# Two VectorE steps of a retrieval stage moved to GpSimd: the normed rows at a tile's beginning, and the add of the normed output into x

## What is computed

```python
x = x + _layernorm(_L1_attn_ref(_layernorm(x, axis=-1), memory, ...), axis=-1)

def _L1_attn_ref(hidden, memory, Wq, Wk, Wv, Wo, log_beta, g_state, b_state, g_mem, b_mem):
    Q = layernorm(hidden, g_state, b_state) @ Wq.T
    ...
    for _ in range(3):
        scores = einsum('bhsd,hnd->bhsn', xi, K) * beta     # 8 heads, 256 memories
        w = entmax15(scores)                                # a threshold per row and head, squared
        xi = einsum('bhsn,hnd->bhsd', w, V)
    return xi.transpose(0, 2, 1, 3).reshape(B, S, H * hd) @ Wo.T
```

## Time and profile before

| | us |
|---|---|
| median of three runs | 1821.33 (1820.55 to 1825.54) |
| the profiled execution | 1821.18, its span 1819.4 |
| busy in the span: PE | 1564.8 (86%) |
| busy in the span: DVE | 1361.7 (75%) |
| busy in the span: ACT | 1150.3 (63%) |
| busy in the span: POOL | 756.4 (42%) |

### The profile page before, as it was taken

How to read it: one execution, slowest core, us unless ns; L and a number is a source line. 1 busy time by engine, 2 the same in 40 slices (tenths; PEclk the granted TensorE clock), 3 DMA queues, 4 the chain that set the end, 5 groups by cost and what they waited for, 6 DMA issues and landing times. The chain is left out here.

```text
span 1819.4 us, 25815 instructions
## 1 busy us (share of the span) xinstructions
PE 1564.8 (86%) x7434; PEld 1099.6 (60%) x7434; DVE 1361.7 (75%) x3568; ACT 1150.3 (63%) x2769; POOL 756.4 (42%) x2049
## 2 busy tenths in 40 slices
PE   5799999999857788887997789877779999999987
PEld 2545657465646667766776678666645556555554
DVE  6665757572359999999999999999644566766646
ACT  3333342412148999899998998899547565665630
POOL 3514224140136776777667776777410101001000
PEclk9799999998988989989998999899889999999989
DMA  5000000000110000000000000000000000000000
GB/s 230 1 1 1 1 1 1 1 1 0 55 57 1 1 1 1 1 1 1 1 1 1 1 1 1 1 1 1 1 0 1 1 1 1 1 13 1 13 1 23
DMA packets 6716, 19.21 MB, mean 11 GB/s; under 512 B 1072, under 2 KB 4144, under 8 KB 5296
## 3 DMA queue, kind: packets, MB, share of 16 engines
q1 hardware_dynamic: 6576, 17.58, 2.6%
HBM read 15.48 MB, written 2.10 MB: 10 GB/s over the span
## 5 line engine op out<-in xcount | busy, mean ns | idle before, releaser
L1361 DVE BATCH_NORM_STATS2 r_moments<-mem_arena 128x6 f32<-128x512 f32 x576 | 382.7, 683 | 4.4 <-ACT mem_arena L1649 4.3
L1649 ACT ACTIVATE mem_arena<-mem_arena,r_shift 128x256 f32<-128x256 f32 x792 | 351.2, 513 | 33.1 <-POOL r_shift L1554 33.1
L1717 PE MATMUL r_bank<-arena,r_wT 128*128 128x256 f32 x1024 | 228.4, 381 | 7.5 <-ACT mem_arena L1649 5.8
L1717 PEld LDWEIGHTS r_bank<-arena,r_wT 128*128 128x128 f32 x1024 | 192.0, 190 | 37.9 <-issue 13.1
L1734 PE MATMUL r_bank<-ident,mem_arena 128*128 128x128 f32 x576 | 107.9, 323 | 90.2 <-DVE mem_arena L1377 89.5
L1734 PEld LDWEIGHTS r_bank<-ident,mem_arena 128*128 128x128 f32 x576 | 81.9, 166 | 127.2 <-DVE mem_arena L1377 97.2
L1325 DVE MAX8 r_top<-r_bank 128x8 f32<-128x256 f32 x384 | 144.2, 416 | 14.5 <-PE r_bank L1717 14.0
L2275 ACT ACTIVATE arena<-arena,e_NM 128x512 f32<-128x512 f32 (+3 forms) x256 | 134.4, 559 | 29.2 <-DVE e_NM L1963 29.2
L1717 PE MATMUL r_bank<-arena,r_xnT 128*128 128x256 f32 x512 | 120.8, 396 | 19.9 <-ACT mem_arena L1649 19.1
L1963 DVE CUSTOM_DVE_ANT_0 arena<-e_banks,mask_q 128x512 f32<-128x512 f32 (+3 forms) x256 | 110.2, 485 | 29.7 <-PE e_banks L2480 29.3
L1361 DVE BATCH_NORM_STATS2 r_moments<-r_u 128x6 f32<-128x512 f32 x192 | 129.2, 684 | 2.8 <-ACT r_u L1649 2.6
(11 more groups left out here) (332 smaller groups left out, 3366.2 us busy)
## 6 DMA issues: line engine op xcount, KB each, us to landing
w<-in_w SPq DMA_DIRECT2D x3, 1024.0 KB, 14.3
out_x<-X SPq DMA_DIRECT2D x4, 512.0 KB, 2.9
X<-in_x SPq DMA_DIRECT2D x1, 1536.0 KB, 10.7
w_in<-in_w_in SPq DMA_DIRECT2D x1, 1156.0 KB, 6.5
mem_arena<-in_wq SPq DMA_DIRECT2D x1, 1024.0 KB, 17.1
mem_arena<-in_wo SPq DMA_DIRECT2D x1, 1024.0 KB, 20.9
gate<-in_gate SPq DMA_DIRECT2D x1, 1024.0 KB, 7.6
up<-in_up SPq DMA_DIRECT2D x1, 1024.0 KB, 9.6
```

The source lines that it names most:

```text
L1361: last = dve.bn_stats(moments[:, a.lane, 2 * p:2 * p + 2, :].rearrange("p two c -> p (two c)"), u[a.lane][:, 2 * p:2 * p + 2, :].rearrange ...
L1649: last = act.activation(u[a.lane][:, h, :], u[a.lane][:, h, :] if k else scores[:, h, :], ACT.Relu, bias=shift[:, a.lane, h:h + 1])
L1717: last = pe.matmul(scores[:, h, :], lhs, (G1 if a.first else G2)[:, h, i, :], start=i == 0, stop=i == 1)
```

## The change

POOL makes the normed rows: `tile_rstd` also makes minus the mean, `tile_rows` multiplies it by the inverse deviation, and one tensor_scalar gives X * rstd + (-mean * rstd). It stands in POOL's slot behind the third head of its weights. For tiles 0 to 11 POOL also adds the normed output into X (`add_rows`), in the same place; DVE still makes the normed output, and it waits for the former tile's add before it writes it. The last four tiles keep their add on DVE. The statistics for the block that follows wait for the first four adds. The semaphore `rstd_ready` goes, `onorm_ready` comes.

```diff
--- before.py
+++ after.py
@@ -1250,11 +1250,13 @@
         ors = sb("r_ors", [P, 1])
         onorm = sb("r_onorm", [P, D])
         one_eps = sb("r_one_eps", [P, 1])
+        minus_one = sb("r_minus_one", [P, 1])
+        off = sb("r_off", [P, LANES])
         eps_sq = sb("r_eps_sq", [P, 1])
 
         ready = sem("ready")
-        stats_ready, rstd_ready, xn_ready, xnT_in_psum, xnT_ready = (sem(n) for n in (
-            "stats_ready", "rstd_ready", "xn_ready", "xnT_in_psum", "xnT_ready"))
+        stats_ready, xn_ready, xnT_in_psum, xnT_ready, onorm_ready = (sem(n) for n in (
+            "stats_ready", "xn_ready", "xnT_in_psum", "xnT_ready", "onorm_ready"))
         scores_done, top_ready, centred, squared, sum2, sum4, sum8, mean_ready, msq_ready, gap_ready, room_ready = (
             sem(n) for n in ("scores_done", "top_ready", "centred", "squared", "sum2", "sum4", "sum8", "mean_ready",
                              "msq_ready", "gap_ready", "room_ready"))
@@ -1307,15 +1309,6 @@
                 dve.drain()
                 dve.bn_aggr(mv[:, a.lane, :], stats[:, a.lane, :]).then_inc(stats_ready, 1)
 
-            def tile_rows(a):
-                if not (a.live and a.first):
-                    return
-                dve.wait_ge(rstd_ready, of_tile(a))
-                if a.tile >= 2:
-                    dve.wait_ge(xnT_in_psum, a.tile - 1)
-                dve.tensor_scalar(xn[:, a.tile % 2, :], X[:, a.tile, :], mv[:, a.lane, 0:1], rstd[:, a.lane:a.lane + 1],
-                                  ALU.subtract, ALU.mult).then_inc(xn_ready, 1)
-
             def largest(a, *heads):
                 if not a.live:
                     return
@@ -1387,11 +1380,17 @@
                 if not (a.live and a.last):
                     return
                 dve.wait_ge(ors_ready, of_tile(a))
-                dve.tensor_scalar(onorm[:], out_rows(a), omv[:, 0:1], ors[:, 0:1], ALU.subtract, ALU.mult)
+                if 0 < a.tile <= ending:
+                    dve.wait_ge(x_ready, a.tile)
+                last = dve.tensor_scalar(onorm[:], out_rows(a), omv[:, 0:1], ors[:, 0:1], ALU.subtract, ALU.mult)
+                if a.tile < ending:
+                    last.then_inc(onorm_ready, 1)
+                    return
                 dve.drain()
                 dve.tensor_tensor(X[:, a.tile, :], X[:, a.tile, :], onorm[:], ALU.add).then_inc(x_ready, 1)
 
             def first_batch_stats():
+                dve.wait_ge(x_ready, TPB)
                 dve.drain()
                 for t in range(TPB):
                     dve.bn_stats(T["e_stats"][:, t, :], X[:, t, :])
@@ -1417,7 +1416,6 @@
                 invert(Unit(n - 6), 2)
                 take_moments(Unit(n - 5), 1, 1, 2)
                 weights(Unit(n - 7), 1, 2)
-                tile_rows(Unit(n - 2))
                 take_moments(Unit(n - 5), 1, 3)
                 invert(Unit(n - 5), 1)
                 weights(Unit(n - 7), 3)
@@ -1453,6 +1451,7 @@
         @block.gpsimd
         def _(pool):
             pool.memset(one_eps[:], 1.0 + EPS)
+            pool.memset(minus_one[:], -1.0)
             pool.memset(eps_sq[:], EPS * EPS)
             pool.memset(inv_n[:], 1.0 / NMEM)
             for k in range(TOP):
@@ -1471,7 +1470,19 @@
                 pool.drain()
                 pool.tensor_tensor(v, v, eps_sq[:], ALU.add)
                 pool.drain()
-                pool.tensor_tensor(rstd[:, a.lane:a.lane + 1], v, T["half_neg"][:, 0:1], ALU.pow).then_inc(rstd_ready, 1)
+                pool.tensor_tensor(off[:, a.lane:a.lane + 1], mv[:, a.lane, 0:1], minus_one[:], ALU.mult)
+                pool.tensor_tensor(rstd[:, a.lane:a.lane + 1], v, T["half_neg"][:, 0:1], ALU.pow)
+
+            def tile_rows(a):
+                if not (a.live and a.first):
+                    return
+                o, r = off[:, a.lane:a.lane + 1], rstd[:, a.lane:a.lane + 1]
+                pool.drain()
+                pool.tensor_tensor(o, o, r, ALU.mult)
+                if a.tile >= 2:
+                    pool.wait_ge(xnT_in_psum, a.tile - 1)
+                pool.drain()
+                pool.tensor_scalar(xn[:, a.tile % 2, :], X[:, a.tile, :], r, o, ALU.mult, ALU.add).then_inc(xn_ready, 1)
 
             def centre(a):
                 if not a.live:
@@ -1568,6 +1579,12 @@
                 pool.tensor_tensor(ove[:], omv[:, 1:2], T["eps"][:, 0:1], ALU.add)
                 pool.drain()
                 pool.tensor_tensor(ors[:], ove[:], T["half_neg"][:, 0:1], ALU.pow).then_inc(ors_ready, 1)
+
+            def add_rows(a):
+                if not (a.live and a.last and a.tile < ending):
+                    return
+                pool.wait_ge(onorm_ready, of_tile(a))
+                pool.tensor_tensor(X[:, a.tile, :], X[:, a.tile, :], onorm[:], ALU.add).then_inc(x_ready, 1)
 
             def first_batch_norms():
                 var, rstd, rms, mv = (T["e_" + n] for n in ("var", "rstd", "rms", "mv"))
@@ -1607,6 +1624,8 @@
                 newton(Unit(n - 3), 0)
                 if n - 5 != UNITS - 1:
                     weights(Unit(n - 5), 7)
+                tile_rows(Unit(n))
+                add_rows(Unit(n - 7))
                 second_moment(Unit(n - 4), 2)
                 centre(Unit(n - 2))
                 square(Unit(n - 2))
```

## The result

| | before | after |
|---|---|---|
| median, us | 1821.42 (4 runs) | 1844.45 (1843.25 to 1845.76, 4 runs) |
| profiled execution, its span | 1821.18, 1819.4 | 1843.7, 1841.9 |
| memory stage: first DVE row to the last add into X | 833.5 | 857.3 |
| busy in the span: DVE | 1361.7 | 1351.1 |
| busy in the span: POOL | 756.4 | 775.2 |

The ratio is 1.0122, 95% interval 1.0105 to 1.014: 23.0 us slower. DVE lost 10.6 us of work and POOL got 18.8, and neither sum is the result.

What follows compares the result with a forecast made beforehand. The bound was POOL's gapless chain from DVE's first moments through `centre`, for which DVE's `clear` waits. Normed rows 19.4, start 5.4 and add net 2.3 made 27.1 us; on 1821.3 that gave 1848.4 us, range 1838 to 1866.

Steps and rivals of the forecast that it cites:

- (a): DVE between maxima and `clear`: removing the normed rows, 0.45 us each, only lengthens a wait for POOL; gain 0.
- (b): POOL before the second moment: normed rows add 1.62 us in each of twelve tiles, 19.4 us slower.
- (c): Start of the memory stage: tile 0's normed rows stand behind four tiles' deviations on POOL; 5.4 us slower.
- (d): DVE before the moments that release POOL: losing the add gains 0.50 us in twelve tiles, 6.0 us.
- (e): POOL's gapless stretch before `centre`: the add costs 0.69 us in twelve tiles, 8.3 us; net of DVE's gain 2.3.
- (f): PE's `output` waits for POOL's add, 2 to 3.7 us; transposes 0.8 us late, room 1.1 us; charged 0.
- Rival 2: PE turns late by the new wait or half clock: 5 to 18 us more, about 1860 us; 18%.
- The first: Rival: DVE is the bound and POOL's added work fits its idle time, 1815.3 us; 3%.
- The third: Rival: two scalars make POOL's normed rows cost 1.75 us instead of 1.14, 1856.3 us; 10%.
- The fourth: Rival: POOL's normed rows partly covered by the maxima, or the ramp overlaps, 1829 us; 7%.
- the fifth: Rival: the work moves without effect, for instance since `clear` waits anyway, 1821 us; 2%.
- What would show it: Signs in the later profile: DVE idle about 2.1 us before `clear`, periods of 17.3 us in slots with normed rows.

Runs made afterwards that it cites:

- rows_in_gap: Normed rows on POOL moved behind `start`, into a POOL wait, add on DVE, against the kernel before the change: ratio 1.0015, 2.7 us slower.
- add_in_gap: Only the add on POOL, moved behind its first head of weights, normed rows on DVE, against the kernel before: 1814.04 us against 1823.92, ratio 0.9948.
- warm_output_half: Changed kernel plus 6 or 3 dummy matmuls on PE ahead of its wait for the add: 1842.17 us, ratio 1.0111 to the kernel before.
- pe_waits_onorm: Changed kernel, but PE's `output` waits for DVE's normed output instead of POOL's add: 1841.27 us, ratio 1.0102 to the kernel before.

## Why the prediction was right

1848.4 us were forecast, 1844.45 came, in the range and with the sign; 27.1 us against 23.0. By its steps:

- **(a) DVE's normed rows give 0**: right, shown by rows_in_gap. I expected the 0.45 us as idle time at `clear` and found them there.
- **(b) normed rows on POOL, 19.4 us**: the mechanism was right, the size was not. This is the term that was mis-sized: 1.62 us per tile, measured 1.07, 12.8 us in all. The step that was off is "I take 1.14, the nearest row". The row was the same engine and shape but had max as its second operation; the true price was 0.55, far nearer to the lower bound of 0.438 than to the upper. 12 x 0.59 us too much from this, 12 x 0.04 too little for the drains.
- **(c) the start, 5.4 us**: 5.3 at the first MAX8, 6.0 by the tenth `clear`. Two errors cancel, which is luck: with the real price PE's first transposes are only 4.8 us later (8.32 us after the stage's start instead of 3.50), and the first scores, at a granted clock of 0.50 instead of 0.60, add 0.46. I had let the clock stand here too. After the first `clear` the next three slots take 0.8 us more than before and the six after them 0.4 less.
- **(d), (e) the add, net 0.19 us per slot**: 0.13 to 0.18 in six of the seven slots that are not long, 0.33 in the seventh. Right, and add_in_gap separates the terms: DVE's 0.50 come back when POOL's 0.69 lie elsewhere. By the Trainium skill, GPSIMD Engine Reference, section When to use GPSIMD, about two times DVE's time was an estimated 0.85; the run has 0.72, 1.7 times.
- **(f) PE's new wait, 0**: wrong in two of nine slots. The waits are 3.1 us in the first of a group and 1.5 in the others, where I had some 3.7 and 2. I compared PE's lateness with its room at full clock and let the clock stand. Rival 2 had it, with 1.5 us in 3 to 12 slots; it was 1.7 in two slots, 3.4 us by warm_output_half. The long wait costs a little at full clock too: 17.55 us in the first group, and 17.37 in pe_waits_onorm, where that wait is gone.
- **The rivals.** The first (DVE is the bound, POOL's work is hidden) is refuted by the changed kernel, but for the add it is right in another place of POOL's order: in add_in_gap POOL's work is hidden and DVE's relief counts. For the normed rows it is right nowhere that was tried: in rows_in_gap POOL's work is hidden too, and DVE's relief gives nothing. The third (two scalars are dear) is refuted by 550 ns. The fourth (partly covered) and the fifth (no effect) by the sums above. The fourth's 1829 also holds (d); (c) and (e) alone, as it is worded, would be 1835.0.
- **What would show it**: I said 17.3 us for the slots with rows, by the price of (b); 16.73 to 17.01 came. I put all of DVE's wait, 2.1 us, at `clear`; 0.39 are there and 1.16 before the moments, through ACT.

So that the number came within 4.0 us is in part luck. (b) alone was 6.6 us too high. What (d), (e) and (f) put at 2.3 was 5.8, which hid half of it. With the true price and the rest as it stands the forecast would have been 1841.8. The slots and stages that belong to no step took 2.2 us off again.

Open: which group is hit. Waits of PE of the same length (3.08 and 3.05 us) are followed by the full clock in one group of tiles and by the low one in the next, in different groups from kernel to kernel, and each kernel was profiled once. That the low clock makes the slot long is shown; what decides that it comes is not. The long waits all stand in one place of the order, so the runs don't separate the length of a wait from its place.

## What to carry to other kernels

On an engine that works through a hand-written list, a third of idle time is not yet room: look at which wait ends where, and put moved work into a wait that is longer than it. Here the same move of the add costs 0.13 to 0.18 us a tile in one place, and more where PE's clock falls behind it, and gives 0.50 in another, a few instructions earlier. Before moving work off the busiest engine, look whether it lies in front of a wait: the normed rows did, and were worth nothing. And when a chain of first elements is turned round by a fixed order (four deviations, then the first rows), charge the whole of it at the start.

## What the runs showed of the hardware

- A tensor_scalar of 128x256 float32 on GpSimd takes 479 ns with mult and a constant add, 549 with mult, add and two scalars per partition, 547 with add, mult, and 1214 with mult, max (medians of 16; 1142 on the mean with add, max in the weights). The operation max makes it more than twice as long; a second scalar adds 70 ns.
- A tensor_tensor add of that shape takes 724 ns on GpSimd and 426 on VectorE (0.43 us in the earlier trace rows).
- Behind 2.0 to 3.7 us of idle TensorE 16 rows of `output` took 5.17 to 6.67 us in 13 of 18 cases and 3.69 in the other 5; behind 1.5 to 1.6 us they took 3.69 in all 36. In the changed kernel the granted clock was 0.68 over one such stretch of 5.3 us, and a row took up to 634 ns instead of 379. With matmuls in the wait the same stretch had 1.00.
